# Rows kept in a buffer of their own between two layers, and a new order of TensorE's fillers in a two-pass expert layer

## The reference, cut to what matters

```
mod = silu(c) @ wmod -> sa, ca, ga, sb, cb, gb          (per layer; ga, gb keep their sign, size at least 0.25)
h = layernorm(x) * (1 + ca) + sa;   x = x + ga * attention(h)
h = layernorm(x) * (1 + cb) + sb;   x = x + gb * experts(h)
```

## Time and profile before

| | us |
|---|---|
| median of 3 runs | 931.58 |
| lowest, highest | 924.52, 932.99 |
| the profiled execution | 933.74 |
| its span in the trace | 930.8 |

### The profile page before, as it was taken

One profiled execution on the slowest core, in us unless ns is written; L12 is line 12 of the kernel. 1 busy time (PEld: TensorE's weight loads), 2 busy tenths in 40 slices (PEclk: granted clock), 3 DMA queues, 4 the chain that ended last, 5 costly groups with the idle time before them and its releaser, 6 DMA issues.

```text
span 930.8 us, 13496 instructions
## 1 busy us (share of the span) xinstructions
PE 789.8 (85%) x4594; PEld 645.8 (69%) x4594; DVE 586.4 (63%) x1346; ACT 444.7 (48%) x975; POOL 248.8 (27%) x180
## 2 busy tenths in 40 slices
PE   4787999989999899998997889999973326999992
PEld 4576788877888778887886787788863123666661
DVE  5547768677686776867785679688892453333333
ACT  3356757657576575766674254246331112333320
POOL 1005201151011610113202356467631003333310
PEclk9979999999999999999999989999995657999997
DMA  4000000100001000002000555456418101111104
GB/s 180 1 14 22 1 1 1 35 24 2 1 1 35 24 1 1 2 1 72 6 1 18 138 179 177 132 159 181 153 38 343 42 23 38 42 44 42 45 13 135
DMA packets 22258, 55.08 MB, mean 59 GB/s; under 512 B 2893, under 2 KB 8398, under 8 KB 21040
## 3 DMA queue, kind: packets, MB, share of 16 engines
q1 hardware_dynamic: 18784, 47.79, 15.4%
q0 software_dynamic: 2208, 5.12, 1.9%
q10 hardware_dynamic: 1200, 1.31, 0.5%
HBM read 49.76 MB, written 5.37 MB: 59 GB/s over the span
## 4 chain that ended last, share of the span: by engine, by line
PE 62%; DVE 24%; DMA 6%; ACT 4%; issue 3%; SPq 1%; POOL 0%; DVEq 0%; POOLq 0%; ACTq 0%
PE ps L1396 12%; PE ps L1397 11%; PE ps L1398 11%; PE ps L1764 9%; PE ps L1503 5%; PE ps L1782 4%; DVE fc L1139 3%; DVE mx L974 2%; DMA wbc<-combine 2%; DMA rows<-xn_h 2%; DVE pT_lo L988 2%; DVE hid_lo L1144 2%; DVE fb L1128 2%; DVE fa L1125 1%; PE ps L1628 1%
## 5 line engine op out<-in xcount | busy, mean ns | idle before, releaser
L680 ACT ACTIVATE prob<-ps,negb,rqs 128x128 f32<-128x128 f32 (+7 forms) x128 | 106.7, 833 | 67.9 <-DVE negb L979 67.1
L669 ACT ACTIVATE pT_hi<-ps 128x512 fp32r<-128x512 f32 (+1 forms) x192 | 88.6, 490 | 60.3 <-PE ps L1503 53.8
L490 POOL TENSOR_TENSOR oT_lo<-o_f,oT_hi 128x512 fp32r<-128x512 f32 x32 | 41.3, 1290 | 284.7 <-ACT oT_hi L755 284.7
L974 DVE TENSOR_REDUCE mx<-ps 128x1 f32<-128x128 f32 (+7 forms) x128 | 96.5, 754 | 22.6 <-PE ps L1495 21.1
L988 DVE TENSOR_TENSOR pT_lo<-ps,pT_hi 128x512 fp32r<-128x512 f32 (+1 forms) x192 | 99.9, 548 | 1.2 <-ACT pT_hi L669 1.1
L1764 PE MATMUL ps<-wgu,xgT 128*128 x184 | 88.3, 604 | 1.0 <-ACT xgT L825 1.0
L1396 PE MATMUL ps<-pT_hi,v_hi 128*128 128x512 f32 x192 | 73.7, 384 | 15.3 <-DVE pT_lo L988 15.3
L1503 PE MATMUL ps<-ident,prob 128*128 128x128 f32 x576 | 85.9, 275 | 0.6 <-DVE qT_lo L1008 0.4
L515 POOL TENSOR_TENSOR w_sp<-w_raw,w_sp 128x768 fp32r<-128x768 f32 x34 | 65.6, 1930 | 56.6 <-ACT w_sp L655 56.6
L1396 PE MATMUL ps<-kT_hi,qT_hi 128*128 128x512 f32 (+1 forms) x192 | 69.9, 364 | 5.4 <-ACT prob L680 3.6
L1398 PE MATMUL ps<-pT_hi,v_lo 128*128 128x512 f32 x192 | 66.8, 348 | 0.0
(11 more groups left out here) (250 smaller groups left out, 2035.9 us busy)
## 6 DMA issues: line engine op xcount, KB each, us to landing
w_raw<-in_ffn SPq DMA_DIRECT2D x34, 384.0 KB, 4.2
wbc<-combine SPq DMA_DIRECT2D x32, 256.0 KB
wgu<-in_gate_up SPq DMA_DIRECT2D x8, 1024.0 KB, 11.6
wdn<-in_down SPq DMA_DIRECT2D x8, 512.0 KB, 7.3
wqkv_raw<-in_w_attn SPq DMA_DIRECT2D x4, 768.0 KB, 4.2
wo_raw<-in_w_out SPq DMA_DIRECT2D x4, 512.0 KB, 3.2
wmod_t<-in_wmod SPq DMA_DIRECT2D x1, 1536.0 KB, 17.9
x<-in_x ACTq DMA_DIRECT2D x1, 1024.0 KB, 7.1
```

The source lines that it names most:

```text
L490: nc.gpsimd.tensor_tensor(oT_lo[:, m % HPG, :], o_f[:], oT_hi[:, m % HPG, :], ALU.subtract).then_inc(oT_lo_done, 1)
L669: nc.scalar.activation(pT_hi[:, unit % NUNITS, 0:nb, qi * P:(qi + 1) * P], ps[:, ROTATING[place % 3], 0:nb * P].rearrange("p (j t) -> p j ...
L680: nc.scalar.activation(prob[:, n % 3, 0:w], ps[:, pair:pair + 2, :].rearrange("p b k -> p (b k)")[:, 0:w], ACT.Exp, bias=negb[:, n % 2:n % ...
L974: nc.vector.reduce_max(mx[:, i:i + 1], ps[:, pair:pair + 2, :].rearrange("p b k -> p (b k)")[:, 0:w], AX.X).then_inc(row_max, 1)
```

## The change

Five things, in the diff below (cut to its core):

1. The rows stored for the last experts, and all of the last layernorm's rows, are written to a buffer of their own, `xn_r` (eight tiles). ScalarE issues the two stores itself (`store_rows`), and no engine waits for them before it writes rows. The first half's last layernorm is finished together with the second half's, after the loop. POOL waits with `x_b` of the second half until VectorE has normalised.
2. Attention's tail: `rows` at steps 130 and 131, `route` at 132, `count` at 135; in each step the output pieces `y` come ahead of `count` and `spread`. `sigmoids` and `expert_weights` move to step 134. `up(0)` moves behind the last output piece.
3. Layer 1's modulation is computed at step -1 of attention, its weights loaded by SP in the beginning, into space that attention uses later; VectorE's part stands at steps 1, 3 and 5.
4. The second half's fillers in the loop come later (normalise u = 3, transposes 5, route 8, count 13, spread 16), and the first half's chain of layer 1 one or two units earlier (statistics u = 18, transposes 22, `state_in` and `scan` 23, `state_out` 25).
5. Behind the loop, TensorE transposes the second half first, the first half's stored rows between `state_in(1)` and `state_out(1)`, and routes the first half after `transpose_state(1)`.

The constants and `bank_plan`; SP; POOL; the helpers of ScalarE:

```diff
-TRANSPOSE_ROWS = (127, 128)
-ROUTE = 130
-COUNT = 133
-FIRST_UP = 134
+TRANSPOSE_ROWS = (130, 131)
+ROUTE = 132
+COUNT = 135
 SPREAD = 136
...
         if n == ROUTE:
             take("route", 0)
+        for half in range(2):
+            p, r = divmod(n - YLAG - half, PHASE)
+            if r == 0 and 0 <= p < PHASES:
+                take("y", 2 * p + half)
         if n == COUNT:
             take("count", 0)
         if n == SPREAD:
             take("spread", 0)
-        for half in range(2):
-            p, r = divmod(n - YLAG - half, PHASE)
-            if r == 0 and 0 <= p < PHASES:
-                take("y", 2 * p + half)
...
             sp.dma_start(wo_raw[:], w_out_d[0]).then_inc(wo_raw_in, 16)
...
             sp.dma_start(svec[:], ssm_vec_d).then_inc(ssm_loaded, 16)
...
                 sp.dma_start(wgu[:, e, :], gate_up_d[:, e, :]).then_inc(w1_loaded, 16)
-
-            rows1 = rows1_d.rearrange("(t p) d -> p t d", p=P)
-            for h in range(2):
-                sp.wait_ge(rows_normed, 16 + 4 * h)
-                if h == 1:
-                    sp.wait_ge(ln_normed, NT + 4)
-                sp.dma_start(rows1[:, 4 * h:4 * h + 4, :], xn_h[:]).then_inc(rows_stored, 16)
-
...
+            pool.wait_ge(ln_normed, NT + 2)
             shifted_rows(1)
...
-            def normalise_rows(k, tiles):
-                act.wait_ge(shift_ready, k + 1)
+            rows1 = rows1_d.rearrange("(t p) d -> p t d", p=P)
+
+            def store_rows(h, act_count):
+                act.wait_ge(rows_normed, act_count)
+                if h == 1:
+                    act.wait_ge(ln_normed, NT + 4)
+                act.dma_start(rows1[:, 4 * h:4 * h + 4, :], xn_r[:, 4 * h:4 * h + 4, :]).then_inc(rows_stored, 16)
+
+            def normalise_rows(shifts, tiles, last=False):
+                act.wait_ge(shift_ready, shifts)
                 for t in tiles:
-                    nc.scalar.activation(xn_h[:, t % 4, :], x[:, t, :], ACT.Identity, bias=shift[:, t:t + 1],
+                    nc.scalar.activation(xn_r[:, t, :] if last else xn_h[:, t % 4, :], x[:, t, :], ACT.Identity, bias=shift[:, t:t + 1],
                                          scale=rs_y[:, t:t + 1]).then_inc(rows_normed, 1)
```

ScalarE in the loop over u and behind it:

```diff
-                if u == 2:
-                    normalise_rows(1, tiles_of(1))
-                if u in (3, 4):
-                    if u == 3:
+                if u == 3:
+                    normalise_rows(2, tiles_of(1))
+                if u in (5, 6):
+                    if u == 5:
                         act.wait_ge(h_lo, 6)
...
+                if u == 11:
                     act.wait_ge(ssm_loaded, 80)
                     nc.scalar.activation(a_t[:], svec[:, 0:1], ACT.Exp).then_inc(a_step, 1)
                     act.wait_ge(a_step, 1)
                     nc.scalar.activation(a_disc[:], a_t[:], ACT.Exp, scale=-1.0).then_inc(a_step, 1)
+                if u == 16:
+                    combine_out(1, SUMS[1])
                 if u == 18:
                     rows_into_sums(1)
-                if u == 20:
+                if u == 19:
                     keep_rows(0)
+                if u == 21:
+                    act.wait_ge(x_kept, 2)
+                    normalise_rows(3, tiles_of(0))
                 if u == 22:
...
                         modulate(2, 1, 0, kc, SUMS[0] + kc)
                 gated_high(u)
 
-            normalise_rows(3, tiles_of(0))
             keep_rows(1)
+            act.wait_ge(x_kept, 4)
+            normalise_rows(4, (6, 7))
+            normalise_rows(4, tiles_of(0), last=True)
+            store_rows(0, 18)
             for kc in range(KC):
-                modulate(3, 1, 4, kc, SUMS[0] + kc)
-            act.wait_ge(x_kept, 4)
-            act.wait_ge(rows_stored, 16)
-            normalise_rows(4, (6, 7))
+                modulate(3, 1, 0, kc, SUMS[1] + kc)
+            act.wait_ge(hc_done, 4)
+            act.wait_ge(z_ready, 4)
+            for kc in range(KC):
+                modulate(4, 1, 4, kc, SUMS[0] + kc)
+            normalise_rows(5, (6, 7), last=True)
+            store_rows(1, 20)
             act.wait_ge(logits_done, 3)
-            for kc in range(KC):
-                modulate(4, 1, 0, kc, SUMS[1] + kc)
-            normalise_rows(5, (6, 7))
             for kc in range(KC):
                 modulate(5, 1, 4, kc, SUMS[1] + kc)
```

VectorE, steps n of attention, then the loop over u and behind it:

```diff
                         capped_weights(0, bank)
                 chain = norm_part_at(n)
                 if chain is not None:
                     norm_part(*chain)
+                rows = ps[:, 1, :].rearrange("p (r d) -> p r d", r=2)
+                if n == 1:
+                    dve.wait_ge(mod_done, 3)
+                    nc.vector.tensor_copy(modc[:, 1, :], ps[:, 3, 0:8])
+                    nc.vector.tensor_scalar(opc[:, 1, :], ps[:, 3, 0:8], 1.0, None, ALU.add)
+                    link(nc.vector.tensor_scalar(gates[:, 2:4, :], rows, 0.0, 2.0, ALU.is_ge, ALU.mult))
+                if n == 3:
+                    link(nc.vector.tensor_scalar(gates[:, 2:4, :], gates[:, 2:4, :], -1.0, None, ALU.add))
+                    nc.vector.tensor_tensor(gabs[:], rows, gates[:, 2:4, :], ALU.mult).then_inc(mod_copied, 1)
+                if n == 5:
+                    dve.wait_ge(mod_copied, 2)
+                    nc.vector.scalar_tensor_tensor(gates[:, 2:4, :], gabs[:], 0.25, gates[:, 2:4, :], ALU.max,
+                                                   ALU.mult).then_inc(gates1_ready, 1)
...
                     shifts(tiles_of(0))
-                if n == 131:
+                if n == 132:
                     chosen_experts(0)
-                if n == 132:
                     expert_flags(0)
+                if n == 134:
+                    sigmoids(0)
+                    expert_weights(0)
...
-                if u == 11:
+                if u == 13:
                     expert_weights(1)
-                if u == 12:
+                if u == 14:
                     capped_weights(1, SUMS[1] + 1)
-                if u == 15:
-                    dve.wait_ge(mod_done, 3)
-                    nc.vector.tensor_copy(modc[:, 1, :], ps[:, SUMS[1], 0:8])
-                    nc.vector.tensor_scalar(opc[:, 1, :], ps[:, SUMS[1], 0:8], 1.0, None, ALU.add)
-                    link(nc.vector.tensor_scalar(sign, rows, 0.0, 2.0, ALU.is_ge, ALU.mult))
                 if u == 16:
-                    link(nc.vector.tensor_scalar(sign, sign, -1.0, None, ALU.add))
-                    link(nc.vector.tensor_tensor(size, rows, sign, ALU.mult))
...
+                if u == 18:
+                    layer_out_stats(0)
                 if u == 19:
-                    layer_out_stats(0)
-                if u == 20:
                     variances(tiles_of(0))
                     root_steps(tiles_of(0), 1)
-                if u == 21:
+                if u == 20:
                     root_steps(tiles_of(0), 2)
                     shifts(tiles_of(0))
-                if u == 25:
+                if u == 23:
                     dve.wait_ge(gates1_ready, 2)
                     scan(0)
-                if u == 26:
+                if u == 25:
                     state_rows(0)
...
                     link(stats(xt, tiles_of(0)))
-                    variances(tiles_of(0))
-                if u == 33:
-                    root_steps(tiles_of(0), 3)
-                    shifts(tiles_of(0))
                 gated_low(u)
 
 
             layer_out_stats(1)
-            variances(tiles_of(1))
-            root_steps(tiles_of(1), 3)
-            shifts(tiles_of(1))
+            variances(range(NT))
+            root_steps(range(NT), 3)
+            shifts(range(NT))
             dve.wait_ge(x_kept, 3)
-            dve.wait_ge(rows_stored, 16)
-            dve.wait_ge(ln_transposed, 12)
             normalise(xt, xn_h, (4, 5))
```

TensorE, steps n, then the loop over u and behind it:

```diff
-                if n == FIRST_UP:
-                    pe.wait_ge(h_lo, 6)
-                    pe.wait_ge(exp_done, STEPS)
-                    up(0)
+                if n == -1:
+                    pe.wait_ge(mod1_loaded, 16)
+                    mod_columns(wmod1, 1, 3, 0, (0, 1))
+                    mod_columns(wmod1, 1, 3, 4, (3, 4))
+                    gate_rows(wmod1, 1, 1).then_inc(mod_done, 1)
+                if n == PHASE:
+                    pe.wait_ge(mod_copied, 2)
...
                 if u == 0:
+                    pe.wait_ge(h_lo, 6)
+                    pe.wait_ge(exp_done, STEPS)
                     mark_banks(0)
+                    up(0)
...
-                if u == 10:
+                if u == 13:
                     count_chosen(1, SUMS[1] + 1)
-                if u == 13:
+                if u == 16:
                     transpose_combine(1, SUMS[1])
-                if u == 14:
-                    pe.wait_ge(mod1_loaded, 16)
+                if u == 18:
                     pe.wait_ge(wT_ready, 2)
-                    mod_columns(wmod1, 1, SUMS[1], 0, (0, 1))
-                    mod_columns(wmod1, 1, SUMS[1], 4, (3, 4))
```

(25 more changed lines are left out.)

69 lines of the change are left out of this document (29 added, 40 removed).

## The result

The changed kernel takes 896.39 us (median of 4 runs, 892.94 to 901.09) against 932.29 us (median of 4, 924.52 to 935.25) of the kernel before: ratio 0.9631, 95% interval 0.9557 to 0.9705 (the ratio is taken over all runs and isn't the quotient of the two medians). A second set of runs on another chip gave 0.9621 (0.9578 to 0.9664). 893 us was predicted. The profiled execution took 895.54 us (span 893.7).

A forecast was written before the change was run, and what follows sets the result against it. It took a transfer queue to bound the stretch between layers, TensorE the expert loop, a transfer the loop's start. Terms summed to 39.0 us: 933.7 to 894.7, 892.6 against the median, taken as 893; range 881 to 909.

The forecast's parts named there:

- (a): Between the layers: last down to router's result falls from 56.1 to 38.3 us, a gain of 17.8 (14 to 20).
- (b): Start of the layer: weight loads issued earlier, so wbc lands sooner and up(4) starts sooner; gain 7.5 us (2 to 10).
- (c): Expert loop: layer 1's modulation leaves it, with the slow clock behind it; gain 6.9 us (5 to 7).
- (d): TensorE's stops inside the expert loop shrink: 3.3 us (1 to 4.5) from later fillers, plus 1.9 from two smaller stops.
- (e): Last units: variances and root steps leave units 32 and 33, so the last down waits less; gain 2.6 us (1.5 to 3.5).
- (f): Attention's start: modulation at step -1 partly hidden in TensorE's 4.79 us wait for k_f; cost 1.0 us (-2 to 3).
- `up(3)` ends within a microsecond of where it did: Start of the layer: moving up(0) behind the output rows would leave the end of up(3) within a microsecond.
- half clock behind the gap: Sign of being wrong: TensorE at half clock over a few us after the 5 us gap, pushing wbc back.
- the loop gives back what it gets: Rival, expert loop: every freed stop returns as a wait for fc or hid_lo; 24.4 us gained, 907 us; chance 13%.
- The rival by which the port lock costs every unit its pace: Rival, expert loop: VectorE's fc and hid_lo blocked beside POOL in every unit; up to 951 us, slower; chance 3%.

The follow-up runs named there:

- e1: The kernel before with only the second rows' own buffer added, stores still on SyncE's queue behind the gate_up loads: ratio 0.9803 (0.9756 to 0.985).
- e2: The kernel before, same buffer, with SyncE's first store of rows issued ahead of the gate_up loads: ratio 0.9799 (0.9749 to 0.9848).
- e11: The kernel before with only attention's end changed: row transposes, routing and count later, up(0) behind the last output rows: ratio 0.9997 (0.9963 to 1.0030).
- e3: The kernel before with only layer 1's modulation moved from unit 14 to step -1: ratio 0.9930 (0.9885 to 0.9975).
- e6: The changed kernel with the second half's fills back at their old units (count 10, spread 13): ratio to the kernel before 0.9648 (0.9591 to 0.9704).
- e7: The changed kernel with VectorE's hid_lo(0) issued ahead of the second half's statistics: 899.09 us, ratio to the kernel before 0.9612.
- e4: The changed kernel with up(0) put back into the stop before attention's last output rows: 895.49 us, ratio to the kernel before 0.9585.
- e8: The changed kernel with up(0) back before the last output rows and hid_lo(0) ahead of the statistics: 895.18 us, ratio to the kernel before 0.9572.
- e5: The changed kernel without GpSimd's wait ahead of the second half's x_b: ratio to the kernel before 0.9654 (0.9592 to 0.9716).
- a_again: The changed kernel run once more, unchanged, beside kernels derived from it: 900.77 us, ratio to the kernel before 0.9621.

## Why the prediction was right, and where it wasn't

| term | predicted | before against changed profile | its own runs |
|---|---|---|---|
| (a) between the layers | 17.8 (14 to 20) | 18.0 | 17.7 in e1 and e2 |
| (b) start of the layer | 7.5 (2 to 10) | 3.0 (1.7 against e2, 5.8 against e1) | about 0; 3.4 at most (e11) |
| (c) modulation | 6.9 (5 to 7) | with (d) 11.8 | 7.6 to 10.3 in its stage (e3) |
| (d) stops | 3.3 + 1.9 | see (c) | 5.6 (e6, without the 1.9) |
| (e) last units | 2.6 (1.5 to 3.5) | 3.1 | none |
| (f) start cost | -1.0 (-3 to 2) | +2.0 | -1.7 to -4.1 |
| sum | 39.0 | 37.1 with -0.9 behind the router | |

In the table (b) is 50.7 - 46.7 less 1.0 for the transposes that moved behind up(4), and (c) with (d) is 148.2 - 137.4 plus the same 1.0.

(a) was right step by step. What the prediction called the cause was only half of it: it said that `xn_h` "is stored on SP's queue behind eight loads of `wgu`, and must not be overwritten before". e2 shows that the first half of that sentence is enough.

(b) is the term that was mis-sized. The step that failed is "`up(3)` ends within a microsecond of where it did", and with it "Then `down(1)` starts at 531.8 and not at 539.2, and `up(4)` at 533.3". Counted from S, the last matmul of up(3) ends at 41.6 us in before and at 45.4 in the changed kernel, 3.8 us later, `down(1)` starts at 45.3 where 40.8 was forecast, and up(4) at 46.7 where 42.2 was. The last matmul of up(3), before and changed:
```profile
532.23 0.40 PE L1398 MATMUL ps<-hT_hi,w_sp 128*128 128x512 f32 x1
```
```profile
534.06 0.40 PE L1397 MATMUL ps<-hT_hi,w_sp 128*128 128x512 f32 x1
```
The premise held: `fc` of unit 1 no longer waited for its combine weights, and the stop of about 5 us before the last output rows came as forecast, 5.16. But I followed the loads and the routing, and not VectorE at unit 0. There `hid_lo(0)` stands behind 1.40 + 0.38 us of statistics and behind `rs_y`, which took 1.84. TensorE waited 2.10 us for it and then ran `down(0)` in 2.32 us where e7 has 1.58. And the price of moving up(0) was put at nothing; e4 puts it at 2.9 us. Both together, e8, are 3.9 of the missing 4.5. Of the signs of being wrong one came, half clock behind the gap (4.7 us of matmuls), but it did not push `wbc` back to a wait. Of the part at unit 0, 1.9 us hang on which way the race of `rs_y` and `hid_lo` with GpSimd's split turns out (e5).

(c) and (d): the loop's sum of 12.1 against 11.8 in the two profiles. Each part's own run gives more (e6's 5.6 us lie above the upper bound of 4.5 that (d) had), so the two parts can't simply be added from these runs; their S to up(33) also holds what else differs there, as e3's shorter wait for `wbc` (2.68 us). The small stops of 1.14 and 0.82 us went as forecast, but one of 1.10 us, for `xn_h` ahead of the first half's transposes, came in their place. The rival "the loop gives back what it gets" needed 3 and 0 here, and falls with e3 and e6.

(e) 3.1 against 2.6, or 1.9 against e1 and e11, which have 9.8 us here with the old code. The stops before the last two `down` fell from 2.15 and 2.79 us to 1.33 and 1.74, and `down(33)` ran wholly at full clock (673.2 to 681.1 has 1.00, where the earlier trace rows has 0.50 at its end).

The cost (f) was put too low, and the first comparison would have hidden it. TensorE's own modulation of layer 0 is the same code in every kernel, yet it takes two times. Before, then e1:
```profile
20.69 3.41 PE L1419 MATMUL ps<-csil,wmod 128*128 128x1 f32 x16
23.96 3.76 PE L1428 MATMUL ps<-wmod,csb 128*128 128x256 f32 x8
```
```profile
20.91 1.97 PE L1418 MATMUL ps<-csil,wmod 128*128 128x1 f32 x16
22.75 1.97 PE L1427 MATMUL ps<-wmod,csb 128*128 128x256 f32 x8
```
These are matmuls at half speed and at full speed, and the trace's list of clock changes agrees: its first entry, full clock, is at 32.9 us in before and at 21.2 us in e1. The half-speed start reaches its last scores some 5 us later: 491.1 against 486.1 to 487.1 of e1, e2 and e11. The changed kernel's first profile had the quick start (1.85 and 1.97), a_again the other (3.41 and 3.76). Like with like: with the quick start S is at 488.8 to 489.0 in four profiles with the move, 1.7 to 3.0 us later; with the slow one at 493.7 to 495.2 in six, e3 among them, 2.7 to 4.1 us later than in before. The forecast was 1.0, at most 3 (of its working, 5.4 less 4.79 is 0.6 and not 0.8). At step -1 the whole of it takes 7.1 us (3.63 + 3.65 with a small overlap):
```profile
37.46 3.63 PE L1419 MATMUL ps<-csil,wmod_t 128*128 128x1 f32 x32
40.95 3.65 PE L1428 MATMUL ps<-wmod_t,csb 128*128 128x256 f32 x8
```
against a cover of 4.79: the eight rows ran at half clock, 0.46 us each, where the eight of layer 0 took 0.25. That leaves 2.3 us, of which 1.7 are seen at `k_f`'s transposes (44.40 against 42.75 in e1); the rest is lost between there and the last scores. One place shows in the windows: from 80.8 to 87.5 us the granted clock is 0.50 in a_again, and 1.00 in before and in the changed kernel's first profile. What makes it fall there stays open.

That the sum of the two profiles, 37.1, came so near 39.0 was luck: before's profile had the slow start and the changed kernel's the quick one. With a_again, which had the slow start too, the terms are 18.1 (a), 3.1 (b), 11.8 (c and d), 3.1 (e) and -3.7 (f), less 0.9 behind the router: 31.5 us of 930.8. No other term paid for the errors of (b) and (f). The median of the runs, in which both starts can occur, came 3.4 us over the forecast, well inside a range that was set by the rivals and not by these terms. The rival by which the port lock costs every unit its pace didn't come about: `hid_lo` has a median of 692 ns over its 34 uses and a longest of 2781. But what the Trainium skill says of that lock (SBUF — State Buffer, "Who interferes with whom", the second one blocks for the whole of the other) is what e5 shows at two places, `rs_t` (2.30 us beside 2.34) and `hid_lo` (2.20 beside 1.86). The stretched `rs_y` has one input and not two; that it is the same lock is inferred from its length and its place beside the split.

Of all kernels run, e8 and e4 have the lowest ratios, 0.9572 and 0.9585 of before, and medians of 895.18 and 895.49 us against 900.77 of the changed kernel beside them; their intervals don't tell them apart.

## What to carry to other kernels

When an engine waits for a store, look first at what stands ahead of it in its queue: moving one issue gave the same 18 us as 8 KB more buffer per partition. Work that is moved out of a gap leaves the gap: price the place it leaves as well as the place it goes to, and follow every in-order queue that uses its result (here ScalarE's `wT` before `th(0)`, VectorE's statistics before `hid_lo(0)`). And before a difference of a few us is credited to a change, compare code that both kernels share, at the start and wherever two engines can meet: here a slow start was worth 5 us and one race 1.9.

## What the hardware showed unasked

- The same 16 + 8 modulation matmuls, from about 20.5 us on, take 7.2 us or 3.9 us from one execution to the next, and the last scores come 5 us later or sooner (S at 491.1 against 486.1 to 487.1). The windows view shows a granted clock of 1.00 there for both, since the trace's list of clock changes begins only at 32.9 or 21.2 us; the durations tell.
- A stop of 5.16 us is followed at once by about 4.7 us of matmuls at half speed (0.41 us each for 256 columns, 0.28 later). A stop of 2.35 us in e4 is followed by 1.2 us at full speed and then by some 3 us at half speed, the changed kernel's stop of 2.10 us by 0.7 us at full speed and then some 3 at half, and a stop of 1.45 us in e5 by none.
- An instruction of 4 elements per partition took 1.84 us instead of 0.17 beside GpSimd's split of 1.83. With the two starting within 0.01 us of each other, it was this instruction or the next that was held, from one execution to the next.
- A DMA issue from ScalarE took 0.37 us in a stretch in which the DMA engines moved 373 GB/s; up to 2 us more than 0.50 had been feared.
